# Window attention with group normalisation: each block of x read once into a ring, three transposes per tile

## The chip, the cores and the metric

The kernel runs on one core of one Trainium2 chip. The metric is the device time of one execution in microseconds (us); the median of the runs is compared. The profile is one further execution, recorded instruction by instruction. Engines: TensorE (PE; its weight loads are PEld), VectorE (DVE), ScalarE (ACT), GpSimd (POOL), and SyncE (SP), which here only issues DMAs.

## The reference, cut to what matters

```python
x: (8, 56, 88, 192) float32                      # batch, height, width, channels
def gn(v, G=32, eps=1e-5):                       # 32 groups of 6 channels, per image
    m, s = mean and variance over (height, width, the 6 channels)
    return (v - m) / sqrt(s + eps)
def attn(y):                                     # windows of 7 x 11 = 77 tokens
    qkv = y @ qkv_w + qkv_b                      # 192 -> 576
    q, k, v = 8 heads of 24
    p = softmax(q k^T / sqrt(24))                # 77 x 77 per head and window
    return (p v) @ proj_w + proj_b
return x + attn(gn(x))
```

## The kernel before

**Tiling.** A block is 14 image rows (two strips of windows) by 88 columns: 112 partitions (`PART`, 8 window columns w times 14 rows r), on each 11 tiles (pixel columns c of a window) of 192 channels. There are 32 blocks, four to an image. A block holds 16 windows, worked on as 8 pairs (`PAIRS`), so 256 pairs (`N_PAIRS`). The tiles of a block are spread over its 8 steps as `STEP_TILES`: three steps with two tiles, five with one.

**Precision.** Values are split into a half-precision high and low part. `x_split` holds for each tile four chunks of 128 columns: high of channels 0 to 127; high of channels 128 to 191 twice; low of channels 0 to 127; low of channels 128 to 191 and 64 ones (for the bias). TensorE transposes the four chunks (L826), ScalarE evicts them to `xT` (L439), and five products (`PASSES`, L701) make q, k or v.

**The loop.** All engines run a loop over slots i (`for i in range(FIRST, END)`), written out in full; each engine's order within a slot is the order of the code, and semaphores tie the engines together. In slot i: TensorE computes the scores of pair i (L758), projects the output of pair step i-16 (L721 on), makes v (L713) and k (L706) of pair i+1, adds the row maxima (L793), computes the transposed scores (L744), makes q of pair i+1, transposes the tiles of step i+10 (L826), and multiplies the probabilities of pair i-1 with v (L731). VectorE makes the row maximum (L632), the output with the residual (L640), the low parts q_lo and k_lo, the reciprocal of the denominators (L654), its share of the next image's statistics (`group_stats`, L495), and q_hi (L660). ScalarE evicts the numerators (L433), xT, x_split (L447), v, k_hi, oT_hi, and makes the exponential (L469), which the scores of the next slot wait for. POOL multiplies numerators and reciprocals (L345), normalises the step i+12 (L356, L358), copies and subtracts for the split of step i+11 (L366, L367), makes oT_lo (L371) and, once an image, the power -0.5 of the variances (L336).

**DMAs.** x is read three times: into `x_stat` for the statistics (L252, L290, L391), into `x_norm` for the normalisation (L383, ScalarE's queue), and into `y_blk` for the residual (L283, SP's queue). Blocks are moved in four pieces (`PIECES`), each an access of all 8 window columns and 14 rows. ScalarE loads x_norm and stores the output (L387) at the end of even slots. SP also carries the denominators: out of the numerators (L264), the reciprocals to DRAM (L269), and back, spread over partitions (four DMAs a slot, L276). The loads for the statistics stand in SP's order behind a wait on `stat_read` (L289).

**Statistics.** Image 0 is done in setup on VectorE (L575 to L592). For image g they run in the loop, with the last steps placed by `M1, DEV, SQ, DEV2, M2, ROOT, NEWTON, RSTD` slots ahead of the image.

Of the kernel before, what the change touches and what calls it, by code (L numbers as in the profile page):

```python
# [7 lines left out]
F16 = mybir.dt.float16  # L8
# [23 lines left out]
TILES = WIN_W  # L32
# [14 lines left out]
STAT_PIECES = [(0, 6), (6, 5)]  # L47
# [10 lines left out]
V_BUFS, NUM_BUFS, DEN_BUFS, INV_BUFS, ROW_BUFS = 4, 8, 4, 4, 8  # L58
# [4 lines left out]
A_HI, B_HI2, A_LO, B_LO1 = range(4)  # L63
STAT = 512 - 4 * GROUPS
HI2, LO, ONE = CH, CH + CB, 2 * CH + CB
# [18 lines left out]

M1, DEV, SQ, DEV2, M2, ROOT, NEWTON, RSTD = 21, 20, 19, 18, 17, 16, 15, 14
# [7 lines left out]
def window_attention(nc, x, qkv_w, qkv_b, proj_w, proj_b, out):  # L93
    x_rows = x.rearrange("b (s r) (w c) d -> (b s) (r w) (c d)", r=ROWS, c=WIN_W)
# [4 lines left out]
    with ExitStack() as ctx:  # L99
# [10 lines left out]
        wA, wB, wB_lo = sb("wA", [CA, 3 * CH]), sb("wB", [128, 3 * CH]), sb("wB_lo", [128, 3 * CH])  # L110
# [11 lines left out]
        x_stat = [sb(f"x_stat{h}", [PART, HALF, CH]) for h in range(2)]  # L122
# [6 lines left out]
        x_norm = [sb(f"x_norm{p}", [PART, TILES, CH]) for p in range(2)]  # L129
        x_split = [sb(f"x_split{p}", [PART, TILES, 4 * CA], F16) for p in range(2)]  # L130
        y_blk = [sb(f"y_blk{p}", [PART, TILES, CH]) for p in range(2)]
# [30 lines left out]
        act_num, act_oT, act_x = sem("act_num"), sem("act_oT"), sem("act_x")  # L162
# [10 lines left out]
        dma_x = [[sem(f"dma_x{p}_{k}") for k in range(len(PIECES))] for p in range(2)]  # L173
        dma_y = [[sem(f"dma_y{p}_{k}") for k in range(len(PIECES))] for p in range(2)]
        dma_out = [[sem(f"dma_out{p}_{k}") for k in range(len(PIECES))] for p in range(2)]
        dma_stat = [sem(f"dma_stat{p}") for p in range(2)]
# [13 lines left out]
        def piece(buf, k):  # L190
            t0, n = PIECES[k]
            return buf[:, t0:t0 + n, :].rearrange("p c d -> p (c d)")

        def piece_of(rows, c, k):
            t0, n = PIECES[k]
            return rows[c, :, :, t0 * CH:(t0 + n) * CH]

        def stat_landed(g):
            return 16 * (2 * min(g + 1, 2) + 4 * max(g - 1, 0))

        def x_step(bufs, s):
            t0, n = STEP_TILES[s % PAIRS]
            return bufs[parity(s)][:, t0:t0 + n, :]

        def xT_tokens(buf, c):
            return xT[buf][:, :, 0:COLS].rearrange("p k (v c r) -> p k v c r", v=WINS, c=WIN_W)[:, :, :, c, :]
# [4 lines left out]
        def xT_psum(bank, c):  # L211
            at = 4 * c * PART
            return bank[:, at:at + 4 * PART].rearrange("p (k v r) -> p k v r", k=4, v=WINS)
# [23 lines left out]
        def _(sp):  # L237
# [3 lines left out]
            sp.dma_start(bp[:, :], proj_b.rearrange("(a c) -> a c", a=1).broadcast_to([128, CH])).then_inc(dma_w, 16)  # L241
            sp.wait_ge(pool_const, 2)
            p_rows = proj_w.rearrange("(j g d) c -> g d j c", g=NG, d=HD)
            for g in range(NG):
                sp.dma_start(p32[ROW_G * g:ROW_G * g + HD, :, :], p_rows[g, :, :, :]).then_inc(dma_rows, 16)
            b_row = qkv_b.rearrange("(a c) -> a c", a=1)
            for row in (CB, CB + ROW_G):
                sp.dma_start(bias_in[row:row + 1, :], b_row).then_inc(dma_rows, 16)
            for h in range(2):
                sp.wait_ge(stat_read, h + 1)  # L250
                for n in range(2):
# [601 lines left out]
```

## Time and profile before

| | us |
|---|---|
| median of 3 runs | 1517.04 |
| lowest, highest | 1514.28, 1531.82 |
| the profiled execution | 1531.71 |
| its span, first to last instruction | 1529.9 |
| mean granted clock of TensorE in it | 0.971 |
| TensorE busy | 1361.8 (89%) |
| VectorE busy | 1047.8 (68%) |
| ScalarE busy | 1025.4 (67%) |
| POOL busy | 977.4 (64%) |
| DMA data moved | 170.36 MB, mean 111 GB/s |

How to read it: busy times are sums over one engine; the granted clock is the share of TensorE's full clock of 2.4 GHz (0.5 is 1.2 GHz). Matmuls are pipelined, so a busy TensorE need not be at its peak. Idle time of an engine costs only where it delays the chain of work that ends last; in this profile 77% of that chain is TensorE's.

### The profile page before, as it was taken

The page shows a single profiled execution, that of the slowest core. Times are in us where ns is not written, and L with a number is a line of the kernel's source. Part 1 is how long each engine was busy: PE and PEld are TensorE (multiplying, and loading weights), DVE is VectorE, ACT ScalarE, POOL GpSimd, SP SyncE. Part 2 cuts the span into 40 slices and gives each one's busy share as a digit, 9 for nine tenths or more (in the row PEclk, how much of TensorE's full clock was granted, in tenths as well). Part 3 has the DMA queues.
Part 4 walks back from the last instruction along what each step waited for, and adds up shares of the span by engine and source line. Part 5 has one row for each costly group of instructions (what it writes and reads, how often), then busy time and mean ns, then how long its engine had stood idle before and what let it go on. Part 6 is the DMA issues. An engine that isn't in the chain of part 4 may idle for free.

```text
span 1529.9 us, 84594 instructions
## 1 busy us (share of the span) xinstructions
PE 1361.8 (89%) x36832; PEld 1210.0 (79%) x36832; DVE 1047.8 (68%) x2227; ACT 1025.4 (67%) x1912; POOL 977.4 (64%) x1532
## 2 busy tenths in 40 slices
PE   0489899999998999999999989998999989999995
PEld 0377788888887888888888878887888878888884
DVE  5677677677766766777667866777667766666662
ACT  1567677766776677776767766776667666767761
POOL 0546766677665766767667776777667576767433
PEclk9999999999999999999999999999999999999997
DMA  7233344444444444444444443544433333433333
GB/s 211 69 95 88 112 114 129 120 118 124 108 128 100 115 129 104 129 107 132 111 114 134 113 108 108 132 123 116 116 99 97 98 95 89 106 95 93 85 84 105
DMA packets 129892, 170.36 MB, mean 111 GB/s; under 512 B 46898, under 2 KB 101490, under 8 KB 128628
## 3 DMA queue, kind: packets, MB, share of 16 engines
q1 hardware_dynamic: 98292, 100.59, 26.8%
q10 hardware_dynamic: 31232, 64.35, 14.0%
q8 instruction: 293, 4.80, 1.3%
q14 instruction: 75, 0.61, 0.1%
HBM read 132.04 MB, written 31.54 MB: 107 GB/s over the span
## 4 chain that ended last, share of the span: by engine, by line
PE 77%; DVE 8%; issue 6%; ACT 3%; POOL 3%; DMA 2%; SPq 1%; ACTq 0%; POOLq 0%; DVEq 0%
PE ps_a L698 13%; PE ps_b L698 13%; PE ps_q L698 11%; PE ps_k L698 11%; PE ps_a L731 10%; PE ps_s L744 8%; PE ps_s L758 5%; PE ps_k L826 4%; PE ps_q L793 3%; DVE neg_max L632 2%; POOL st_root L336 2%; DVE stat L495 2%; ACT probs L469 1%; DMA bias_in<-in_qkv_b 1%; DVE st_dev L510 1%
## 5 line engine op out<-in xcount | busy, mean ns | idle before, releaser
L632 DVE TENSOR_REDUCE neg_max<-ps_s 77x16 bf16<-77x1232 f32 x256 | 369.6, 1444 | 221.9 <-PE ps_s L758 221.1
L371 POOL TENSOR_TENSOR oT_lo<-o,oT_hi 128x308 f16<-128x308 f32 x256 | 193.7, 756 | 321.1 <-ACT oT_hi L463 321.1
L469 ACT ACTIVATE probs<-ps_s,exp_shift,exp_scale 77x1232 f32<-77x1232 f32 x256 | 349.2, 1364 | 9.9 <-PE ps_s L744 9.1
L731 PE MATMUL ps_a<-probs,v_all 77*32 77x77 f32 x8192 | 200.6, 234 | 41.1 <-issue 39.8
L452 ACT ACTIVATE v_all<-ps_a 77x384 f32<-77x384 f32 x256 | 124.9, 488 | 166.5 <-PE ps_a L698 166.4
L698 PE MATMUL ps_a<-wv_hiA,xT 128*128 128x192 f16 x1024 | 218.7, 253 | 2.5 <-issue 1.8
L345 POOL TENSOR_TENSOR o<-num,inv_all 128x308 f32<-128x308 f32 x256 | 216.2, 845 | 4.7 <-DMA inv_all<-den_dram 4.7
L439 ACT ACTIVATE xT<-ps_k 128x448 f16<-128x448 f16 x347 | 209.5, 642 | 8.9 <-PE ps_k L826 8.9
L731 PEld LDWEIGHTS ps_a<-probs,v_all 77*32 77x32 f32 x8192 | 148.7, 110 | 68.8 <-issue 44.4
L698 PE MATMUL ps_b<-wp_hi,oT_hi 128*112 128x192 f16 x694 | 188.1, 271 | 13.0 <-POOL oT_lo L371 6.8
L433 ACT ACTIVATE num<-ps_a 128x308 f32<-128x308 f32 x256 | 109.3, 427 | 133.0 <-PE ps_a L731 118.6
L698 PE MATMUL ps_k<-xT,wqk_hiA 128*128 128x154 f16 x1024 | 193.5, 236 | 0.0
L698 PE MATMUL ps_q<-xT,wqk_hiA 128*128 128x154 f16 x1024 | 186.0, 235 | 0.4 <-issue 0.3
L645 DVE TENSOR_TENSOR q_lo<-ps_q,q_hi 128x308 f16<-128x308 f32 x256 | 123.1, 481 | 89.4 <-PE ps_q L793 86.4
L649 DVE TENSOR_TENSOR k_lo<-ps_k,k_hi 128x308 f16<-128x308 f32 x256 | 123.1, 481 | 87.6 <-ACT k_hi L458 86.7
L458 ACT ACTIVATE k_hi<-ps_k 128x308 f16<-128x308 f32 x256 | 110.1, 430 | 106.5 <-PE ps_k L698 106.5
L698 PE MATMUL ps_b<-wp_lo,oT_hi 128*112 128x192 f16 x694 | 177.3, 255 | 0.2 <-issue 0.2
L698 PE MATMUL ps_b<-wp_hi,oT_lo 128*112 128x192 f16 x694 | 177.5, 256 | 0.0
L358 POOL TENSOR_TENSOR x_norm<-x_norm,rstd_all 112x384 f32<-112x384 f32 (+1 forms) x248 | 162.7, 656 | 19.4
L367 POOL TENSOR_TENSOR x_split<-x_norm,x_split 112x384 f16<-112x384 f32 (+1 forms) x248 | 170.2, 686 | 0.0
L356 POOL TENSOR_TENSOR x_norm<-x_norm,mean_all 112x384 f32<-112x384 f32 (+1 forms) x248 | 163.2, 658 | 4.1 <-issue 4.1
L366 POOL COPY x_split<-x_split 112x128 f16<-112x128 f16 (+1 forms) x248 | 64.1, 258 | 155.2 <-ACT x_split L447 154.8
(148 smaller groups left out, 3854.9 us busy)
## 6 DMA issues: line engine op xcount, KB each, us to landing
inv_all<-den_dram SPq DMA_DIRECT2D x1024, 38.5 KB
x_stat<-in_x SPq DMA_DIRECT2D x24, 504.0 KB, 6.1
x_norm<-in_x ACTq DMA_DIRECT2D x32, 336.0 KB
x_norm<-in_x ACTq DMA_DIRECT2D x64, 168.0 KB
y_blk<-in_x SPq DMA_DIRECT2D x32, 336.0 KB
y_blk<-in_x SPq DMA_DIRECT2D x64, 168.0 KB
out<-y_blk ACTq DMA_DIRECT2D x32, 336.0 KB
out<-y_blk ACTq DMA_DIRECT2D x64, 168.0 KB
```

The source lines that it names most:

```text
L345: nc.gpsimd.tensor_tensor(o32[o % 2][:, :], num[o % NUM_BUFS][:, :], inv_all[o % INV_BUFS][:, :], ALU.mult)\
L356: nc.gpsimd.tensor_tensor(x4, x4, of_group(mean_all, g, tiles), ALU.subtract).then_inc(pool_centred, 1)
L358: nc.gpsimd.tensor_tensor(x4, x4, of_group(rstd_all, g, tiles), ALU.mult).then_inc(pool_norm, 1)
L367: nc.gpsimd.tensor_tensor(xs[:, :, LO:ONE], x_step(x_norm, x_s), xs[:, :, 0:CH], ALU.subtract)\
L371: nc.gpsimd.tensor_tensor(oT_tokens(oT_lo, o), by_column(o32[o % 2]), oT_tokens(oT_hi, o), ALU.subtract).then_inc(pool_oT, 1)
L439: last = nc.scalar.activation(xT_tokens(parity(x_s), t0 + c), xT_psum(x_bank(x_s), c), ACT.Copy)
L452: nc.scalar.activation(v_all[v % V_BUFS][:, :, 0:HD], ps_a[0:TOK, 0:2 * CH].rearrange("p (h d) -> p h d", d=HD), ACT.Copy)\
L469: nc.scalar.activation(probs[i % 2][:, :, :].rearrange("p g (a n) -> p g a n", a=4), scores(), ACT.Exp, bias=exp_shift[0:TOK, :], scale=ex ...
L632: nc.vector.tensor_reduce(neg_max[:, :, :, HD:HD + 1].rearrange("p a g e -> p g (a e)"), scores(), AXIS.X, ALU.max, negate=True).then_inc( ...
L645: tt(heads(q_lo), heads(ps_q), heads(q_hi), ALU.subtract).then_inc(dve_q, 1)
L698: last = mm(dst, lhsT, rhs, start=first and n == 0, stop=n == len(pairs) - 1, skip_group_check=True)
L731: last = mm(o, v_all[s % V_BUFS][:, HEADS * w + NG * j + g, :], probs[s % 2][:, g, at:at + TOK], start=True, stop=True, skip_group_check=True)
```

## The change

x is loaded once, by window columns, into `x_ring`, a ring of 11 blocks. Statistics, normalisation and residual all read the ring; the output is added in place and stored from it, by columns, the last block by pieces as before. `x_norm` and `x_split` shrink to three buffers of one step each. `x_split` has three chunks of 128: high of channels 0 to 127; high and low of channels 128 to 191; low of channels 0 to 127. The fourth chunk of `xT` has its 64 rows of ones set once in setup, and POOL copies the 64 rows of the high part into it from the second chunk, after ScalarE's eviction. The steps of the statistics move by up to a slot; square and second moments share one. In setup the weights' DMAs are put in another order, and VectorE normalises step by step; POOL's first step waits for it.

```diff
+RING, STEP_BUFS = 11, 3
+LOAD_LEAD = 8 * RING - 27
-V_BUFS, NUM_BUFS, DEN_BUFS, INV_BUFS, ROW_BUFS = 4, 8, 4, 4, 8
+V_BUFS, NUM_BUFS, DEN_BUFS, INV_BUFS, ROW_BUFS = 3, 8, 4, 4, 8
-A_HI, B_HI2, A_LO, B_LO1 = range(4)
+A_HI, B_BOTH, A_LO, B_ONE = range(4)
-        for h, first in ((0, base - 53), (1, base - 37)):
+        for h in range(2):
             for n in range(GROUPS):
-                at = first + n // 2 if g > 1 else (h * GROUPS + n) // 5 - 3
+                at = base - 47 + n // 2 if h == 0 else base - 31 + n // 3
+                if g == 1:
+                    at = (h * GROUPS + n) // 5 - 3
-M1, DEV, SQ, DEV2, M2, ROOT, NEWTON, RSTD = 21, 20, 19, 18, 17, 16, 15, 14
+M1, DEV, SQ, DEV2, M2, ROOT, NEWTON, RSTD = 20, 19, 18, 18, 17, 16, 15, 14
+        def column(c, w):
+            return x_ring[ROWS * w:ROWS * (w + 1), c % RING, :, :].rearrange("p c d -> p (c d)")
+        def ring_step(s):
+            t0, n = STEP_TILES[s % PAIRS]
+            return x_ring[:, s // PAIRS % RING, t0:t0 + n, :]
...
@@ SP
+            def load_x(c, w):
+                sp.dma_start(column(c, w), x_blk[c, w, :, :]).then_inc(dma_x[c % RING], 16)
+            for c in range(BLOCKS_IMG):
+                for w in range(NWC // 2, NWC):
+                    load_x(c, w)
+            sp.wait_ge(dma_x[2], landed(2))
+            for c in range(BLOCKS_IMG, 2 * BLOCKS_IMG):
+                for w in range(NWC):
+                    load_x(c, w)
...
-                c, r = divmod(i - 5, PAIRS)
-                if r % 2 == 0 and 0 <= c < BLOCKS:
...
-                        sp.wait_ge(stat_read, 2 * g + h - 1)
...
+                c, r = divmod(i + LOAD_LEAD, PAIRS)
+                if r < NWC // 2 and 2 * BLOCKS_IMG <= c < BLOCKS:
+                    reach(sp, dma_out[c % RING][r // 2], NWC // 2 * 16 * (c // RING))
+                    load_x(c, 2 * r)
+                    load_x(c, 2 * r + 1)
@@ GpSimd
+                    if n == PAIRS:
+                        pool.wait_ge(dve_x0, PAIRS)
-                    nc.gpsimd.tensor_tensor(x4, x4, of_group(mean_all, g, tiles), ALU.subtract)
+                    nc.gpsimd.tensor_tensor(x4, raw, of_group(mean_all, g, tiles), ALU.subtract)
...
-                    nc.gpsimd.tensor_copy(xs[:, :, HI2:LO], xs[:, :, CA:CH])
-                    nc.gpsimd.tensor_tensor(xs[:, :, LO:ONE], x_step(x_norm, x_s), xs[:, :, 0:CH], ALU.subtract)
+                    minus(xs[:, :, CH:LO_A], xn[:, :, CA:CH], xs[:, :, CA:CH])
+                    minus(xs[:, :, LO_A:], xn[:, :, 0:CA], xs[:, :, 0:CA]).then_inc(pool_x, 1)
+                x_s = i - 1 + X_LEAD
+                if exists(x_s):
+                    pool.wait_ge(act_xT, x_s + 1)
+                    t0, n = STEP_TILES[x_s % PAIRS]
+                    by_tile = xT[parity(x_s)][0:CB, :, 0:COLS].rearrange("p k (v c r) -> p k v c r", v=WINS, c=WIN_W)
+                    nc.gpsimd.tensor_copy(by_tile[:, B_ONE, :, t0:t0 + n, :], by_tile[:, B_BOTH, :, t0:t0 + n, :]).then_inc(pool_xT, 1)
@@ ScalarE
+            for c in range(BLOCKS_IMG):
+                for w in range(NWC // 2):
+                    nc.scalar.dma_start(column(c, w), x_blk[c, w, :, :]).then_inc(dma_x[c % RING], 16)
...
-                c, r = divmod(i + 18, PAIRS)
-                if r % 2 == 0 and 2 <= c < BLOCKS:
-                    load_x(c, r // 2)
+                c, r = divmod(i - P_LAG - PAIRS, PAIRS)
+                if r < NWC // 2 and 0 <= c < BLOCKS - 1:
+                    act.wait_ge(dve_out, PAIRS * (c + 1))
+                    store_column(c, 2 * r)
+                    store_column(c, 2 * r + 1)
@@ VectorE
-                last = nc.vector.bn_stats(stat6[g % 2][:, h, n, :], x_stat[h][:, :, GCH * n:GCH * (n + 1)])
+                a, b = sorted((one % RING, two % RING))
+                last = nc.vector.bn_stats(stat6[g % 2][:, h, n, :], x_ring[:, a:b + 1:b - a, :, GCH * n:GCH * (n + 1)])
...
+            normalise(0)
+            normalise(1)
+            for step in range(2, PAIRS):
+                split_low(step - 2)
+                normalise(step)
...
-                    if r % 2 == 0:
-                        dve.wait_ge(dma_y[parity(r)][r % PAIRS // 2], 16 * (r // PAIRS // 2 + 1))
-                    y = x_step(y_blk, r)
+                    y = ring_step(r)
@@ TensorE
-            PASSES = ((A_HI, "hiA"), (A_HI, "loA"), (A_LO, "hiA"), (B_HI2, "B"), (B_LO1, "Bb"))
+            PASSES = ((A_HI, "hiA"), (A_HI, "loA"), (A_LO, "hiA"), (B_BOTH, "B"), (B_ONE, "Bb"))
+                    reach(pe, pool_xT, min(v // PAIRS * PAIRS + PAIRS, N_PAIRS))
-                        for chunk in range(4):
+                        for chunk in range(3):
```

## Rows read from the trace of the kernel before

**Rows 1.** Waits of TensorE, 160 to 1373 us: total, times, longest.
```profile
PE ps_a L731 <- issue: 35.6, 25, 3.7
PE ps_s L758 <- ACT probs L469: 12.0, 7, 2.1
```
**Rows 2.** The same view, 1379 to 1486 us; this is its only line.
```profile
PE ps_s L758 <- ACT probs L469: 1.4, 7, 0.2
```
**Rows 3.** Timeline of VectorE, four row maxima (slots 16, 232, 240, 248): start, duration.
```profile
159.52 1.45 DVE L632 TENSOR_REDUCE neg_max<-ps_s 77x16 bf16<-77x1232 f32 x1 [3.51 <-PE ps_s L758]
...
1373.39 1.44 DVE L632 TENSOR_REDUCE neg_max<-ps_s 77x16 bf16<-77x1232 f32 x1 [3.39 <-PE ps_s L758]
...
1415.68 1.44 DVE L632 TENSOR_REDUCE neg_max<-ps_s 77x16 bf16<-77x1232 f32 x1 [0.86 <-PE ps_s L758]
...
1456.16 1.44 DVE L632 TENSOR_REDUCE neg_max<-ps_s 77x16 bf16<-77x1232 f32 x1 [0.73 <-PE ps_s L758]
```
**Rows 4.** Busy time by stretches; last three: granted clock, DMA share, GB/s.
```profile
160.00:1373.00 1213.00, 1137.64 (x31056) 1016.71 (x31054) 847.57 (x1752) 852.83 (x1592) 835.32 (x1303) 0.98 0.43 113
1379.60:1486.00 106.40, 104.85 (x3000) 93.87 (x2992) 73.62 (x127) 74.81 (x136) 55.83 (x89) 1.00 0.36 89
```
**Rows 5.** The same view: start of an odd slot, then two stretches of setup.
```profile
624.60:628.35 3.75, 3.75 (x105) 3.49 (x106) 2.93 (x6) 2.82 (x7) 2.22 (x6) 1.00 0.54 163
22.00:28.00 6.00, 0.00 (x0) 0.00 (x0) 5.86 (x28) 0.00 (x0) 0.39 (x1) 1.00 0.53 196
7.00:14.00 7.00, 0.00 (x0) 0.00 (x0) 0.00 (x0) 0.00 (x0) 0.00 (x0) 1.00 1.03 281
```
**Rows 6.** Timeline, 622 to 631 us: an x_norm load's issue and a TensorE pause.
```profile
622.94 0.70 ACTq L383 DMA_DIRECT2D x_norm<-in_x  x1
...
630.72 0.47 PE L731 MATMUL ps_a<-probs,v_all 77*32 77x77 f32 x16 [1.75 <-issue]
```
**Rows 7.** The page's DMA queues, the instruction queue: packets, MB, share.
```profile
q8 instruction: 293, 4.80, 1.3%
```
**Rows 8.** Timeline of TensorE: scores that begin two slots, transposes of two and one tile.
```profile
456.56 0.32 PE L758 MATMUL ps_s<-k_hi,q_hi 25*128 25x77 f16 x16
460.35 0.56 PE L826 MATMUL ps_k<-ident,x_split 112*128 112x112 f16 x8
461.51 0.32 PE L758 MATMUL ps_s<-k_hi,q_hi 25*128 25x77 f16 x16
...
628.34 0.36 PE L826 MATMUL ps_k<-ident,x_split 112*128 112x112 f16 x4
...
1471.75 0.32 PE L758 MATMUL ps_s<-k_hi,q_hi 25*128 25x77 f16 x16 [0.20 <-ACT probs L469]
...
1476.59 0.32 PE L758 MATMUL ps_s<-k_hi,q_hi 25*128 25x77 f16 x16 [0.20 <-ACT probs L469]
```
**Rows 9.** Groups by shape, POOL: busy us, mean ns, idle before.
```profile
L367 POOL TENSOR_TENSOR x_split<-x_norm,x_split 112x192 f16<-112x192 f32 x155 | 85.1, 549 | 0.0
L367 POOL TENSOR_TENSOR x_split<-x_norm,x_split 112x384 f16<-112x384 f32 x93 | 85.1, 915 | 0.0
L366 POOL COPY x_split<-x_split 112x64 f16<-112x64 f16 x155 | 36.9, 238 | 100.7 <-ACT x_split L447 100.4
```
**Rows 10.** Timeline of VectorE around second moments (slots 110, 111), and the square.
```profile
683.56 0.78 DVE L515 TENSOR_TENSOR st_sq<-st_dev 112x128 f32<-112x128 f32 x1
...
688.39 1.23 DVE L519 SCALAR_TENSOR_TENSOR st_dev<-st_sq,stat 112x64 f32<-112x64 f32 x2
689.54 1.43 DVE L632 TENSOR_REDUCE neg_max<-ps_s 77x16 bf16<-77x1232 f32 x1
```
**Rows 11.** Timeline of VectorE in setup: its first reduction.
```profile
21.71 0.35 DVE L559 TENSOR_REDUCE big_parts<-wA 128x1 f32<-128x192 f32 x1 [15.74 <-DMA bias_in<-in_qkv_b]
```
**Rows 12.** Waits of SP's queue: total, times, longest.
```profile
SPq L290 <- DVE stat L495: 24.9, 1, 24.9
```
**Rows 13.** The chain that ended last, in the tail: a load issued by SP.
```profile
1496.80 0.73 SPq L283
```

More of the change, by code:

```diff
@@ L127, in window_attention @@
         st_dev, st_sq = sb("st_dev", [PART, 2, GROUPS, 2]), sb("st_sq", [PART, 2, GROUPS, 2])
-        x_norm = [sb(f"x_norm{p}", [PART, TILES, CH]) for p in range(2)]
-        x_split = [sb(f"x_split{p}", [PART, TILES, 4 * CA], F16) for p in range(2)]
-        y_blk = [sb(f"y_blk{p}", [PART, TILES, CH]) for p in range(2)]
+        x_ring = sb("x_ring", [PART, RING, TILES, CH])
+        x_norm = [sb(f"x_norm{p}", [PART, 2, CH]) for p in range(STEP_BUFS)]
+        x_split = [sb(f"x_split{p}", [PART, 2, 3 * CA], F16) for p in range(STEP_BUFS)]
         xT = [sb(f"xT{p}", [128, 4, COLS + PAD], F16) for p in range(2)]
@@ L172, in window_attention @@
         dma_inv_all = [sem(f"dma_inv_all{p}") for p in range(INV_BUFS)]
[L173 to L176, printed above, removed]
+        dma_x = [sem(f"dma_x{p}") for p in range(RING)]
+        dma_out = [[sem(f"dma_out{p}_{k}") for k in range(2)] for p in range(RING)]
+        dma_last = sem("dma_last")
         dma_w, dma_rows, dma_bias = sem("dma_w"), sem("dma_rows"), sem("dma_bias")
@@ L240, in _ @@
             sp.dma_start(wB[CB:128, :], qkv_w[CA:CH, :]).then_inc(dma_w, 16)
-            sp.dma_start(bp[:, :], proj_b.rearrange("(a c) -> a c", a=1).broadcast_to([128, CH])).then_inc(dma_w, 16)
             sp.wait_ge(pool_const, 2)
+            b_row = qkv_b.rearrange("(a c) -> a c", a=1)
+            for row in (CB, CB + ROW_G):
+                sp.dma_start(bias_in[row:row + 1, :], b_row).then_inc(dma_rows, 16)
             p_rows = proj_w.rearrange("(j g d) c -> g d j c", g=NG, d=HD)
@@ L245, in _ @@
                 sp.dma_start(p32[ROW_G * g:ROW_G * g + HD, :, :], p_rows[g, :, :, :]).then_inc(dma_rows, 16)
[L246 to L251, printed above, removed]
-                    sp.dma_start(x_stat[h][:, n * TILES:(n + 1) * TILES, :].rearrange("p c d -> p (c d)"),
-                                 x_rows[BLOCKS_IMG + 2 * h + n, :, :]).then_inc(dma_stat[h], 16)
+            sp.dma_start(bp[:, :], proj_b.rearrange("(a c) -> a c", a=1).broadcast_to([128, CH])).then_inc(dma_w, 16)
+            def load_x(c, w):
[7 more added lines that the diff above has]
+                    load_x(c, w)
             sp.wait_ge(dve_bp, 1)
@@ L305, in _ @@
                                     base=0, pattern=[[-1, 128]], channel_multiplier=1).then_inc(pool_const, 1)
-            for p in range(2):
-                nc.gpsimd.memset(x_split[p][:, :, ONE:], 1.0)
             pool.wait_ge(weights_big, 1)
@@ L492, in group_stats @@
             def group_stats(g, h, n):
+                one, two = BLOCKS_IMG * g + 2 * h, BLOCKS_IMG * g + 2 * h + 1
                 if n == 0:
-                    dve.wait_ge(dma_stat[h], stat_landed(g))
-                last = nc.vector.bn_stats(stat6[g % 2][:, h, n, :], x_stat[h][:, :, GCH * n:GCH * (n + 1)])
+                    dve.wait_ge(dma_x[one % RING], landed(one))
+                    dve.wait_ge(dma_x[two % RING], landed(two))
+                a, b = sorted((one % RING, two % RING))
+                last = nc.vector.bn_stats(stat6[g % 2][:, h, n, :], x_ring[:, a:b + 1:b - a, :, GCH * n:GCH * (n + 1)])
                 if n == GROUPS - 1:
```

130 lines of the change are left out of this document (48 added, 82 removed).

## The prediction

> **What bounds the kernel now.** I read the waits of TensorE first, then the starts of one recurring instruction, then busy time by stretches, then single instructions. The loop handles one pair of windows per slot, 256 slots.
>
> TensorE's waits from 160 to 1373 us [rows 1] are mostly "issue": time in which it waited for no engine, 35.6 us inside the attention product alone. In a later stretch the only wait left is 1.4 us for the exponential [rows 2]. The two stretches run the same loop. The starts of VectorE's row maximum give the price [rows 3]. Slots 16 to 232 (27 blocks of eight) take 1373.39 - 159.52 = 1213.9 us, 44.96 us a block. The block from slot 240 takes 1456.16 - 1415.68 = 40.5 us. So the middle loses 27 x 4.46, about 120 us, against a pace that the same engines keep later. The granted clock says the same [rows 4]: 0.98 against 1.00.
>
> What ended near 1373 us? ScalarE's loads into x_norm (L383) stop, after slot 236. Even before, each even slot ended with two DMAs on ScalarE's queue, a load and a store. Their data moves in the following odd slot [rows 5]: the first row is the first 3.75 us of an odd slot, DMA share 0.54. The second row is a stretch of setup with x_norm loads alone: 0.53 and 196 GB/s, flat. The third has the statistics' long rows and reaches 1.03 and 281 GB/s. So the block-shaped DMAs occupy about half of the 16 engines and hold those for long. An example of the cost [rows 6]: the load is issued at 622.94, and TensorE stands still 1.75 us in the attention product ending at 630.72, "issue". The instruction queue fetches 293 packets, 4.80 MB, 16 KB each [rows 7], about one per 4.6 us, which is TensorE's own code. In the packet records the fetches of TensorE's code that come late all start in odd slots. **My reading:** a fetch waits behind the x burst on its DMA engine; TensorE runs dry; after long pauses it resumes at 1.2 GHz for a while.
>
> The Trainium skill ("DMA: Bandwidth & Descriptors", section "Why a DMA increments its semaphore by 16 and not by 1") says a DMA from SP or ACT uses the largest k up to 16 dividing the slowest dimension on both sides. For x_norm, y_blk and out that dimension is 8 in DRAM, so k = 8; by that rule, the 0.53 agrees. For the new column DMAs of 14 rows it gives 14.
>
> **The change, part by part**, against the profiled execution's own 1531.7 us (span 1529.9 and 1.8 around it).
>
> 1. *x traffic.* Three reads of x become one; loads and stores become columns of 14 rows of 8448 bytes, two per slot: stores in slots 0 to 3 of a block, loads in slots 3 to 6. A slot then moves 236 KB, where an odd slot now moves 420 to 504 KB from ScalarE's queue and 168 to 336 KB from SP's. Of the 120 us, two parts are no fetches: POOL's power instruction delays the exponential once an image (12.0 us in seven waits, [rows 1], and an estimated 8 more for the 1.2 GHz stretch that follows the pause), and VectorE's statistics steps some 8 us. About 91 us remain. The later stretch has stores and y loads only, 336 KB or less per burst, and loses nothing. The new bursts are smaller still. Bounds: 0 saved (bursts are not the cause) and 91. I take 79, leaving 12. **-79 us.**
>
> 2. *Three transposes per tile.* In a two-tile slot eight transposes take 0.56 and in a one-tile slot four take 0.36 [rows 8], so 0.05 each. But one-tile slots gain nothing: between 1471.75 and 1476.59 no transposes are left, TensorE waits 0.20 us for the exponential, and the slot still is 4.84 us, as it is with four. There the exponential ends last. A slot with eight transposes, 456.56 to 461.51, takes 4.95, 0.11 above that bound, so two fewer save the whole 0.096. 91 x 0.096: **-9 us** (bounds 0 and 352 x 0.05 = -18). ScalarE's shorter eviction (336 for 448 columns) is followed by idle time in the slot: nothing.
>
> 3. *POOL.* Old per step: copy 0.24 for 64 elements, subtraction 0.55 for 192, 0.92 for 384 [rows 9], so 1.9 ns an element above 0.18 fixed. New: two subtractions, 0.31 + 0.43 for one tile, 0.43 + 0.67 for two, and the copy out of the transposed chunk, 112 or 224 half-precision elements on 64 partitions. No row has this copy; bounds 0.24 and 0.18 + 224 x 1.9 ns = 0.61, I take 0.28 and 0.38, near the old copy, whose kind it is. POOL's busiest slots come to 4.8 us with all its work, inside slots of 4.83 to 4.96. It covers itself, and its late product has 2.7 us of slack before ScalarE needs it. Cover gone: 0.5 us in 31 blocks. The copy waits for ScalarE's eviction, which comes in the same slot earlier than the x_split POOL waits for already; behind it only oT_lo is queued. TensorE's new wait for the copy, once a block at the v projection, is met a slot before: **0.**
>
> 4. *Statistics.* Square and second moments share one slot now. VectorE's second moments (1.23 us) already make the next row maximum late: it starts 0.65 after the scores instead of 0.37 [rows 10]. Adding 0.78 for the square puts this whole amount on the path, seven times (bounds 0 and twice this, should the clock fall): **+6.** Three group statistics per slot instead of two in eleven slots add 0.21 before q_hi, whose slack before the next scores is 0.23 by the starts in the trace: 0.
>
> 5. *Setup.* VectorE's first reduction waits until 21.71 us for the bias rows [rows 11], which share the engines with 5.5 MB of x. Now 1.9 MB stand beside the weights. At 281 GB/s [rows 5], 2.7 MB take 9.7 us; with 2 us of start and 2 of landing, 14.5. Statistics then find blocks 0 and 1 landed. **-7** (0 to -10). POOL must now wait with the second block's three two-tile steps (two instructions each, near the 0.92 of [rows 9]) until VectorE is done, though VectorE itself finishes earlier: **+2** (-2 to +5). The extra memsets sit in the idle 15 us.
>
> 6. *SP's early wait.* SP stood 24.9 us behind the statistics before a load [rows 12], so the first denominators came late and slots 4 and 5 stretched by 3 us. Gone: **-3** (0 to -3). SP's new waits are for stores issued two slots before; behind them stand the denominators, with about 8 us of slack. Its issue work in the loading slots is 2.6 us + two columns at 0.3 to 0.73: under 4.1 of 4.8.
>
> 7. *Tail.* No y load between the last denominators, 0.73 each [rows 13]: **-2** (0 to -5). ScalarE issues two column stores where it issued a load and a store: 0.
>
> Sum: -79 - 9 + 6 - 7 + 2 - 3 - 2 = -92, so 1440 us. The median of the runs is 1517, about 15 below the profiled run; I hold that this is a lighter share of the same stalls, which vanish anyway (64 instead of 79). That gives 1517 - 77 = **1440** too.
>
> **Rivals.**
>
> *The idle is not the bursts.* Then only parts 2 to 7 count: -13, **1504 us.** For it: the fetch packets themselves are short even at stalls, so what I call a queue is a start that comes late, and no row shows what it queued behind. Against: rows 2 and 3. The Trainium skill ("Runtime: NRT & Kernel Launch", section "Instruction fetch mechanics") holds that crossing a 16 KB boundary is mostly hidden; by it this rival is the likely case. The trace speaks against: 35.6 us of pauses. Chance 0.12.
>
> *Half of it.* Bursts in seven slots of eight, with 8448-byte packets, still make some fetches late: 35 to 40 us stay instead of 12, **1466 us.** Chance 0.14.
>
> *Slower: every slot gets a burst.* If a fetch is held by the size of the packets before it and not by the burst's length, late fetches move from half of the slots to seven eighths, and today's 91 us become 160: 1504 + 69 = **1573 us.** It decides from the point where one slot's 236 KB hold a fetch about 2 us or more. Against it: setup's 8448-byte rows move at 281 GB/s, so 236 KB are through in 1 us. Chance 0.05.
>
> *POOL's copy costs its upper bound or more,* late at block borders: +15, **1455.** Inside the forecast's case.
>
> **From cases to numbers.** Forecast 0.69, 1425 to 1460. A measurement of this kernel can tell about 2% from no change, 30 us: faster is below 1487, slower above 1547. Faster: 0.69 + 0.14, less some scatter, 0.81. Same: the first rival and scatter, 0.13. Slower 0.06. The range goes from 1418 (all of 91 saved, setup at its bound) to 1492, leaving out the first rival and the slower one.
>
> **What would show it.** "Issue" waits of TensorE under 15 us; clock 0.99 or more in the middle; blocks of about 41 us throughout; a first reduction near 14.5 us; the one-tile slot still 4.83; POOL's busy time up about 60 us with no wait for it; the slot after the second moments 0.8 longer. Wrong it would be if "issue" stays at 50 us with the DMA share lower.

## The result and the profile after

The changed kernel takes 1452.31 us (median of 4 runs, 1450.42 to 1455.38) against 1520.55 for the kernel before beside it (4 runs, 1514.28 to 1531.82): a ratio of 0.9545, 95% interval 0.9483 to 0.9608. It is faster; the prediction was 1440, in a range of 1418 to 1492. A median is over all runs of a kernel and a ratio over those within 1.5% of its fastest, so beside the widely scattered kernel before of 1525.22 us, below, the two do not divide out. The profiled execution has a span of 1450.9 us against 1529.9, 79.0 less.

The page: span, busy time by engine, DMA queues, HBM.

```profile
span 1450.9 us, 84355 instructions
...
PE 1321.5 (91%) x36480; PEld 1174.7 (81%) x36480; DVE 1049.3 (72%) x2239; ACT 987.0 (68%) x1910; POOL 1027.8 (71%) x1786
...
q10 hardware_dynamic: 7872, 32.18, 12.6%
q8 instruction: 291, 4.77, 1.4%
...
HBM read 71.49 MB, written 31.54 MB: 71 GB/s over the span
```

TensorE's code is still 4.8 MB in some 290 fetches, as in [rows 7]. The queue q10, on which ScalarE's DMAs run, carries 32 MB: the stores and 1.9 MB of x in setup, without the loads of x_norm. The waits of TensorE from 160 to 1373 us (total, times, longest) answer to [rows 1]:

```profile
PE ps_s L757 <- ACT probs L464: 16.0, 11, 2.3
PE ps_q L793 <- DVE neg_max L633: 6.2, 17, 0.6
PE ps_s L743 <- issue: 2.3, 8, 0.4
PE ps_k L826 <- issue: 1.2, 3, 0.6
PE ps_a L730 <- issue: 1.0, 3, 0.5
```

"Issue" summed over all lines of this view was 56.0 us before and is 6.3 now. What is left at the top is the wait for the exponential, which POOL's power delays (halving the power, below, takes it from 16.0 to 5.7). Busy time by stretches (last three: granted clock, DMA share, GB/s), as in [rows 4]:

```profile
160.00:1373.00 1213.00, 1176.95 (x32826) 1052.42 (x32823) 899.80 (x1848) 874.21 (x1695) 929.05 (x1609) 0.99 0.36 75
```

In the same 1213 us TensorE does 32,826 matmuls where it did 31,056. The row maxima of slots 16, 232, 240 and 248, as in [rows 3] (timeline of VectorE: start, duration, idle before):

```profile
155.89 1.44 DVE L633 TENSOR_REDUCE neg_max<-ps_s 77x16 bf16<-77x1232 f32 x1 [0.35 <-PE ps_s L757]
...
1295.49 1.45 DVE L633 TENSOR_REDUCE neg_max<-ps_s 77x16 bf16<-77x1232 f32 x1 [0.76 <-PE ps_s L757]
...
1336.37 1.44 DVE L633 TENSOR_REDUCE neg_max<-ps_s 77x16 bf16<-77x1232 f32 x1 [0.76 <-PE ps_s L757]
...
1376.86 1.44 DVE L633 TENSOR_REDUCE neg_max<-ps_s 77x16 bf16<-77x1232 f32 x1 [0.73 <-PE ps_s L757]
```

The middle takes 1139.6 us in 27 blocks, 42.21 a block where it was 44.96. The late block takes 40.49, as before.

To say where the 79.0 us came from, I give each slot a floor, the 15th percentile of the slots with the same place in a block, and call the rest its excess. Before to after, profiled runs:

| stretch | before | after | difference | predicted |
|---|---|---|---|---|
| to the scores of slot 0 | 71.9 | 74.3 | +2.4 | -5 |
| floors of slots 0 to 254 (40.54 to 40.21 a block) | 1292.3 | 1281.9 | -10.4 | -9 |
| excess, slots 0 to 15 | 6.1 | 0.8 | -5.3 | -3 |
| excess, slots 16 to 231 | 119.4 | 53.9 | -65.5 | -73 |
| excess, later slots | 1.7 | 1.6 | 0 | 0 |
| last scores to the end | 38.6 | 38.4 | -0.2 | -2 |
| sum | 1529.9 | 1450.9 | -79.0 | -92 |

### The profile page after: what moved, and what is told of

Read it like the earlier page. It is cut to its first block, busy times and chain, and to the rows that moved or that the text cites. A ratio compares the mean times of both kernels' runs of the same rounds, so it can differ in the third digit from the quotient of the medians.

```text
span 1450.9 us, 84355 instructions
## 1 busy us (share of the span) xinstructions
PE 1321.5 (91%) x36480; PEld 1174.7 (81%) x36480; DVE 1049.3 (72%) x2239; ACT 987.0 (68%) x1910; POOL 1027.8 (71%) x1786
## 4 chain that ended last, share of the span: by engine, by line
PE 77%; DVE 10%; POOL 4%; ACT 3%; issue 3%; DMA 2%; SPq 1%; ACTq 0%; POOLq 0%; DVEq 0%
PE ps_a L697 13%; PE ps_b L697 13%; PE ps_q L697 12%; PE ps_k L697 11%; PE ps_a L730 9%; PE ps_s L743 8%; PE ps_s L757 5%; DVE neg_max L633 3%; PE ps_q L793 3%; PE ps_k L826 3%; POOL st_root L331 3%; ACT probs L464 2%; DVE stat L495 2%; DMA x_ring<-in_x 1%; DVE q_hi L659 1%
## 5 line engine op out<-in xcount | busy, mean ns | idle before, releaser
L313 POOL TENSOR_TENSOR x_split<-x_norm,x_split 112x128 f16<-112x128 f32 (+1 forms) x496 | 205.8, 436 | 67.1 <-ACT x_split L442 66.8
L697 PE MATMUL ps_a<-wv_hiA,xT 128*128 128x192 f16 x1024 | 213.2, 248 | 6.5 <-ACT num L428 3.4
L730 PE MATMUL ps_a<-probs,v_all 77*32 77x77 f32 x8192 | 194.6, 233 | 1.5 <-issue 1.4
L697 PE MATMUL ps_b<-wp_hi,oT_hi 128*112 128x192 f16 x694 | 184.1, 265 | 13.0 <-POOL oT_lo L373 7.5
L697 PE MATMUL ps_b<-wp_hi,oT_lo 128*112 128x192 f16 x694 | 173.3, 250 | 0.1
L697 PE MATMUL ps_b<-wp_lo,oT_hi 128*112 128x192 f16 x694 | 173.2, 250 | 0.0
L434 ACT ACTIVATE xT<-ps_k 128x336 f16<-128x336 f16 x347 | 168.3, 524 | 5.3 <-PE ps_k L826 5.3
L352 POOL TENSOR_TENSOR x_norm<-x_ring,mean_all 112x384 f32<-112x384 f32 (+1 forms) x248 | 161.5, 651 | 1.4 <-DVE x_split L613 1.4
L458 ACT ACTIVATE oT_hi<-o 128x308 f16<-128x308 f32 x256 | 117.6, 459 | 27.7 <-POOL o L340 27.7
```

The lines of the kernel that those rows point to most:

```text
L313: return nc.gpsimd.tensor_tensor(out, a, b, ALU.subtract)
L352: nc.gpsimd.tensor_tensor(x4, raw, of_group(mean_all, g, tiles), ALU.subtract).then_inc(pool_centred, 1)
L434: last = nc.scalar.activation(xT_tokens(parity(x_s), t0 + c), xT_psum(x_bank(x_s), c), ACT.Copy)
L697: last = mm(dst, lhsT, rhs, start=first and n == 0, stop=n == len(pairs) - 1, skip_group_check=True)
L730: last = mm(o, v_all[s % V_BUFS][:, HEADS * w + NG * j + g, :], probs[s % 2][:, g, at:at + TOK], start=True, stop=True, skip_group_check=True)
```

## The experiments

Two theories of the 56 us of issue waits stood after the result. **T** (the prediction's): the x traffic in flight at once holds TensorE's code fetches. **Q**: what holds them is two transfers back to back on ScalarE's one queue, a load of x_norm and a store, whatever the other queues move; the ring removes this pair because its loads are SP's. Q came up during the first experiments, whose expectations do not name it. In the kernel before, ScalarE issues the load 0.74 us before the store (median of 108 pairs in the timeline). Behind the load of [rows 6] at 622.94 comes:

```profile
623.68 0.69 ACTq L387 DMA_DIRECT2D out<-y_blk  x1
```

So the pair is close in two ways, on one queue and in time, and an edit can change both at once. The first two kernels start from the one before.

**The load of x_norm one slot later than the store.**

```diff
-                c, r = divmod(i + 18, PAIRS)
+                c, r = divmod(i + 17, PAIRS)
```

> The kernel before with one number changed: ScalarE issues its x_norm loads at the end of odd slots, no longer in the same slot as the output's stores. Bytes, sizes and all other instructions are the same. Theory (TensorE's code fetches wait behind the x bursts, and a burst of load plus store is too long): the load now meets SP's y load and the store stands alone, so the longest burst is shorter; the idle called issue falls from 56 us to 10 to 35, the time to 1460 to 1500. Rival one (it is the amount of x traffic that counts): no change, 1512 to 1525. Rival two (the idle has nothing to do with these DMAs): no change either.

Measured: 1483.63 us, ratio to before 0.9679 (0.9616 to 0.9741); issue waits 21.3 us in all. Not a byte less is moved, and 48 us are gone, inside the range of the first theory. So the number of bytes is not it; how they meet is. T and Q both expect this.

**No load of x_norm at all.** Blocks 2 to 31 are normalised from what lies in the buffer; the reading of x for that is left out, and POOL's waits for it.

```diff
...
-                c, r = divmod(i + 18, PAIRS)
-                if r % 2 == 0 and 2 <= c < BLOCKS:
-                    load_x(c, r // 2)
```

> The kernel before without the x_norm loads of blocks 2 to 31: it leaves out reading x for the normalisation, so those blocks normalise what is already in the buffer; all engine instructions stay. Theory: what remains are store bursts and y loads as in the later stretch of before that lost nothing, so issue idle falls under 15 us and the time by 60 to 90 us, to 1430 to 1460. Rival one (amount of traffic): x traffic falls by a quarter, so at most a quarter of the loss goes, 1495 to 1505. Rival two (not these DMAs): 1512 to 1525.

Measured: 1472.90 us, 0.9596 (0.9538 to 0.9655); issue waits 17.3 us. That is 59 us less, little more than moving the load gave, and above the 1430 to 1460 that the theory expected.

**The old shape in the new kernel.** Loads by SP and stores by ScalarE are the old four pieces, in even slots; `load_piece` is the old access into the ring.

```diff
-                if r < NWC // 2 and 2 * BLOCKS_IMG <= c < BLOCKS:
-                    reach(sp, dma_out[c % RING][r // 2], NWC // 2 * 16 * (c // RING))
-                    load_x(c, 2 * r)
-                    load_x(c, 2 * r + 1)
+                if r % 2 == 0 and 2 * BLOCKS_IMG <= c < BLOCKS:
+                    reach(sp, dma_out[c % RING][r // 4], 2 * 16 * (c // RING))
+                    load_piece(c, r // 2)
...
```

> The changed kernel with its in-loop loads and stores in the old form: four pieces a block over all 8 window columns, one load by SP and one store by ScalarE in each even slot, into and out of the ring. x is still read once and the bytes are those of the changed kernel. Theory (the shape and length of the burst count): 500 KB bursts on half of the DMA engines are back in one slot of two, issue idle rises from about 10 us to 30 to 60 and the time by 30 to 70 us, to 1480 to 1520. Rival one (the amount, three reads against one, counts): as the changed kernel, 1448 to 1458.

Measured: 1459.38 us, 0.952 (0.9465 to 0.9575); issue waits 10.5 us. With pieces as long as before, in every second slot, the stalls stay away, and the 30 to 60 us of the theory are missed. The columns' shape is not what helps in the loop. But the burst of load and store is not back as it was: SP issues its load a median of 3.2 us after ScalarE's store, as here:

```profile
617.05 0.67 ACTq L391 DMA_DIRECT2D out<-x_ring  x1
619.92 0.74 SPq L253 DMA_DIRECT2D x_ring<-in_x  x1
```

**The same, with the loads on ScalarE's queue.** Only the slot numbers and the call are shown.

```diff
-                c, r = divmod(i + 66, PAIRS)          # in SP's loop
-                    load_piece(c, r // 2)
+                c, r = divmod(i + 66, PAIRS)          # in ScalarE's loop, ahead of the store
+                    load_piece(c, r // 2)
```

> The changed kernel, but each block's load and store are both issued by ScalarE's queue, back to back in the same even slot, as the old four pieces. Against the run before it (loads by SP, stores by ScalarE, the same pieces in the same slots, 1459 us) only the queue of the loads is different; the bytes are the same. Theory Q (two transfers on ScalarE's one queue hold up what comes behind them, TensorE's program fetches among it): the code stalls come back, issue waits of 20 to 45 us between 160 and 1373 us, 1480 to 1510 us. Theory T (what counted is the x traffic in flight at once, of which the ring leaves two thirds out): the same as with SP's loads, 1455 to 1465 us, issue waits under 12 us.

Measured: 1485.24 us, 0.969 (0.9641 to 0.974), with the unedited changed kernel on the same chip at 1461.87. Waits of TensorE, 160 to 1373 us:

```profile
PE ps_s L742 <- issue: 11.6, 8, 2.8
...
PE ps_k L825 <- issue: 4.1, 5, 1.8
PE ps_q L696 <- issue: 3.8, 2, 2.2
```

28.5 us of issue in all, single pauses of up to 2.8 us. Same bytes, same pieces, same slots of the program: 23 us more than the changed kernel. The time and the issue waits lie in Q's ranges and not in T's. Half of the old stalls come back, not all. But the queue is not all that changed. The load is now issued 0.74 us before the store (median of 87 pairs):

```profile
624.51 0.70 ACTq L381 DMA_DIRECT2D x_ring<-in_x  x1
625.25 0.69 ACTq L387 DMA_DIRECT2D out<-x_ring  x1
```

So this run shows that the pair makes stalls, and not whether by its one queue or by its two bursts falling together.

**The changed kernel again.** No edit.

> The changed kernel once more, unedited, so that the others can be set against it on one chip. All theories: 1452 us (1446 to 1462), a ratio to before of 0.950 to 0.958, issue waits of TensorE of some 6 us in all between 160 and 1373 us.

Measured: 1461.87 us (1457.21 to 1465.37), 0.9531 (0.948 to 0.9583); issue waits 7.0 us. On this chip both kernels run longer, by 1.1% and 0.7%; the ratio is the same within its interval.

**The kernel before, without the loads of y_blk.** VectorE's waits for them go too; the output of blocks 2 to 31 adds what lies in the buffer.

```diff
-                if r % 2 == 0 and 0 <= c < BLOCKS:
+                if r % 2 == 0 and 0 <= c < 2:
...
```

> The kernel before, with the loads of y_blk taken out for blocks 2 to 31, which leaves out re-reading x for the residual of those blocks (they add what lies in the buffer). ScalarE's queue keeps only the stores, SP keeps the loads of x_norm and x_stat. Theory Q (load and store back to back on ScalarE's queue): the pair is gone, stalls fall as with the loads alone removed elsewhere or more, 1450 to 1475 us. Theory T (total traffic at once): x_norm's load in the same slots was worth 47 to 59 us when moved or left out, and y_blk's is as large, so 1465 to 1490 us. If instead only SP's load in the slots of ScalarE's pair mattered (theory S), nothing changes: 1515 to 1530 us.

Here I had named the queues wrongly. y_blk is loaded by SP, in odd slots; x_norm and the store are ScalarE's pair, and this kernel keeps that pair whole. What I wrote for Q and S rests on that mix-up, and that the time fell in S's range says nothing. Read rightly, Q expects the stalls to stay. T's sentence stands: a load as large is gone, 1465 to 1490 us. Measured: 1516.74 us, 0.9899 (0.9845 to 0.9953). Waits of TensorE, 160 to 1373 us:

```profile
PE ps_a L732 <- issue: 29.4, 24, 2.5
...
PE ps_s L759 <- issue: 3.8, 3, 2.0
PE ps_k L827 <- issue: 3.1, 3, 2.3
```

43.1 us of issue in all. To leave out y_blk is worth 1%, to leave out x_norm, as many bytes, 4%. T's range is missed, and bytes per slot are not the measure. In the kernel before, y_blk's load is issued a median of 3.1 us ahead of the store; the pair is what this kernel keeps, close in time and on one queue.

**The kernel before, with the loads of x_norm on SP's queue.** Same slots of the program, same bytes; ScalarE's three lines go.

```diff
                 # SP, behind the load of y_blk
+                c, r = divmod(i + 18, PAIRS)
+                if r % 2 == 0 and 2 <= c < BLOCKS:
+                    k = r // 2
+                    if c == 2:
+                        sp.wait_ge(dve_x0, 2 * k + 2)
+                    reach(sp, pool_x, PAIRS * (c - 3) + 2 * k + 2)
+                    sp.dma_start(piece(x_norm[c % 2], k), piece_of(x_blk, c, k)).then_inc(dma_x[c % 2][k], 16)
```

> The kernel before, with one edit: the loads of x_norm are issued by SP's queue instead of ScalarE's, in the same even slots; bytes, pieces and buffers stay, ScalarE's queue keeps the stores. Theory Q (a load and a store back to back on ScalarE's queue hold up TensorE's program fetches): few late fetches are left, issue waits under 20 us between 160 and 1373 us, 1470 to 1490 us. Theory T (the x traffic in flight at once counts, on whatever queue): stalls stay, issue waits of 45 to 65 us, 1515 to 1535 us.

Measured: 1484.05 us (1471.96 to 1500.44), with a widely scattered kernel before beside it (1525.22, 1494.39 to 1551.21), so 0.9846 (0.9702 to 0.9989). Its profile is of the fastest of its four runs. Waits, then the stretch:

```profile
PE ps_s L748 <- issue: 3.9, 4, 1.9
PE ps_a L735 <- issue: 3.7, 6, 1.4
PE ps_s L762 <- issue: 3.2, 4, 1.6
```

```profile
160.00:1373.00 1213.00, 1177.37 (x32743) 1055.13 (x32742) 887.15 (x1826) 900.28 (x1679) 875.28 (x1374) 0.99 0.47 118
```

13.6 us of issue in all, at 118 GB/s, more than the 113 of [rows 4]. All the traffic is there, and TensorE does 32,743 matmuls in the stretch, nearly the changed kernel's 32,826. The median and the issue waits lie in Q's ranges, and neither the traffic as a whole nor its rate makes the stalls. Whether it is the queue, this run does not say either, because the load has moved in time as well: a median of 3.5 us behind the store.

```profile
617.76 0.67 ACTq L394 DMA_DIRECT2D out<-y_blk  x1
622.74 0.73 SPq L290 DMA_DIRECT2D x_norm<-in_x  x1
```

The stalls that remain speak for time. In the three kernels without the pair, SP still issues x_stat loads of 420 to 504 KB, and 21 stores in each have one within 2 us. In the 7 us behind such a store TensorE has 0.47, 0.27 and 0.45 us of issue (load moved by a slot, on SP's queue, left out); behind the other 91 or 92 stores it has 0.06, 0.04 and 0.06. These are two queues, which suggests that one queue is not needed for a stall. The changed kernel has no such loads. On the other side, y_blk's smaller loads do little even when they are the nearest and within 1 us: 0.09 us behind 15 stores. This is counted from the timelines, not tested by an edit. An SP load issued right beside the store would part T, in the narrow form of two bursts at once, from Q; it was not run.

**Four transposes in the changed kernel.** `x_split` has its fourth chunk again, and POOL copies within `x_split` as before.

```diff
-                        for chunk in range(3):
-                            at = (3 * c + chunk) * PART
+                        for chunk in range(4):
+                            at = (4 * c + chunk) * PART
...
```

> The changed kernel with the fourth chunk transposed again by TensorE and evicted by ScalarE, and POOL copying the 64 high columns inside x_split; everything else as changed. Theory: the three transposes save only in the two-tile slots, so going back costs 91 times 0.1, 9 us: 1460 to 1463. Rival (all 352 transposes lie on the path, at 0.05 each): 18 us, 1470. Second rival (POOL's copies out of the transposed chunk cost more than they save): no change or faster, 1445 to 1453.

Measured: 1458.23 us, 0.951 (0.9454 to 0.9566), the same ratio as the changed kernel's within the interval, and between the ranges that I had given. The floor goes back to 40.54 a block, but the excess of slots 16 to 231 is 49.3 us where the changed kernel has 53.9 and, in its second run, 56.4. So of 10.4 us that three transposes take off the floors, no more can be seen in the total than the scatter of these runs.

**Statistics apart.**

```diff
-                at = base - 47 + n // 2 if h == 0 else base - 31 + n // 3
+                at = base - 48 + n // 2 if h == 0 else base - 32 + n // 3
-M1, DEV, SQ, DEV2, M2, ROOT, NEWTON, RSTD = 20, 19, 18, 18, 17, 16, 15, 14
+M1, DEV, SQ, DEV2, M2, ROOT, NEWTON, RSTD = 21, 20, 19, 18, 17, 16, 15, 14
```

> The changed kernel, but its statistics are read one slot earlier and square and second moments stand in slots of their own, as in the kernel before. Theory (the shared slot costs 0.8 us seven times): 5 to 7 us less than the changed kernel, 0.5% at most. Rival (another wait in that slot hides it): within 2 us of it.

Measured: 1452.45 us, 0.9666 (0.9598 to 0.9734; the scattered kernel before of this chip stands in the ratio). The excess of the five slots with statistics, summed over the six images whose statistics lie between slots 16 and 231, is 12.1 us, against 13.7 and 13.3 in the changed kernel's two runs: 1 to 2 us, so the rival is right. The timelines of VectorE show a difference that fits; the changed kernel first, this one second:

```profile
655.04 0.84 DVE L515 TENSOR_TENSOR st_sq<-st_dev 112x128 f32<-112x128 f32 x1
655.91 0.61 DVE L519 SCALAR_TENSOR_TENSOR st_dev<-st_sq,stat 112x64 f32<-112x64 f32 x2
656.45 1.43 DVE L633 TENSOR_REDUCE neg_max<-ps_s 77x16 bf16<-77x1232 f32 x1
```

```profile
650.49 0.85 DVE L515 TENSOR_TENSOR st_sq<-st_dev 112x128 f32<-112x128 f32 x1
...
655.31 1.30 DVE L519 SCALAR_TENSOR_TENSOR st_dev<-st_sq,stat 112x64 f32<-112x64 f32 x2
656.54 1.43 DVE L633 TENSOR_REDUCE neg_max<-ps_s 77x16 bf16<-77x1232 f32 x1
```

Behind the square the second moments take 0.61 us; alone in a slot they take 1.30. Square and moments make 1.45 together, not the 2.0 of [rows 10] that I had added up.

**The power in two halves.** POOL does 16 of the 32 groups in each of two slots; VectorE's step behind it waits for both.

```diff
-M1, DEV, SQ, DEV2, M2, ROOT, NEWTON, RSTD = 20, 19, 18, 18, 17, 16, 15, 14
+M1, DEV, SQ, DEV2, M2, ROOT, NEWTON, RSTD = 20, 19, 18, 18, 17, 16, 14, 13
-                nc.gpsimd.tensor_tensor(st_root[:, :], st_var[:, :], half_power[:, :], ALU.pow).then_inc(pool_root, 1)
+                nc.gpsimd.tensor_tensor(st_root[:, half], st_var[:, half], half_power[:, half], ALU.pow).then_inc(pool_root, 1)
...
```

> The changed kernel, but POOL's power -0.5 of the variances, 5.4 us in one instruction once an image, is done in two halves in two successive slots, and what follows it stands one slot later. Theory (the power delays POOL's late product and with it ScalarE's numerators and exponential; slots 17 and 18 of an image now cost 24 us over their floor in all seven images, and a half of 2.7 us fits into the slack): 18 to 24 us less than the changed kernel, 1434 to 1442 us where that has 1458, and the waits of TensorE's scores for the exponential fall from 16 us to under 4. Rival (a half still breaks the chain, now in two slots): 0 to 8 us less.

Measured: 1464.26 us, 0.9726 (0.9635 to 0.9818). A miss: no gain, and 12 us more than the kernel with the statistics apart that ran beside it. The exponential's waits do fall, from 16.0 to 5.7 us, but a new one takes their place. Waits of TensorE, 160 to 1373 us, and then VectorE and POOL in the slot behind the second half:

```profile
PE ps_q L795 <- DVE neg_max L635: 19.9, 22, 2.1
PE ps_s L759 <- ACT probs L466: 5.7, 9, 0.9
```

```profile
512.98 3.22 DVE L537 TENSOR_TENSOR newton<-st_root 112x32 f32<-112x32 f32 x1
516.23 0.56 DVE L538 TENSOR_TENSOR newton<-newton,st_var 112x32 f32<-112x32 f32 x1
516.83 1.44 DVE L635 TENSOR_REDUCE neg_max<-ps_s 77x16 bf16<-77x1232 f32 x1
```

```profile
514.10 0.76 POOL L374 TENSOR_TENSOR oT_lo<-o,oT_hi 128x308 f16<-128x308 f32 x1
514.82 0.84 POOL L341 TENSOR_TENSOR o<-num,inv_all 128x308 f32<-128x308 f32 x1
515.62 0.52 POOL L353 TENSOR_TENSOR x_norm<-x_ring,mean_all 112x192 f32<-112x192 f32 x1
516.23 0.52 POOL L355 TENSOR_TENSOR x_norm<-x_norm,rstd_all 112x192 f32<-112x192 f32 x1
```

A product of 112x32 elements, 0.19 us in setup, takes 3.22 (3.02 to 3.31 in the seven images) while POOL, catching up after its half, works without a pause; it ends as POOL passes from one instruction to the next. The row maximum stands behind it. VectorE's small step in another slot is the next thing to try; it was not run.

**Blocks 0 to 3 loaded as pieces.** 112 partitions in one transfer, blocks 0 and 1 by ScalarE, 2 and 3 by SP.

```diff
-                for w in range(NWC // 2):
-                    nc.scalar.dma_start(column(c, w), x_blk[c, w, :, :]).then_inc(dma_x[c % RING], 16)
+                for k in range(len(PIECES)):
+                    nc.scalar.dma_start(ring_piece(c, k), block_piece(c, k)).then_inc(dma_x[c % RING], 16)
...
```

> The changed kernel, but the first four blocks are loaded as pieces of several window columns (112 partitions in one transfer) instead of 16 columns each of 14 partitions; blocks 0 and 1 by ScalarE's queue, 2 and 3 by SP's. Theory: the columns reach only 148 GB/s in the setup against 196 GB/s for pieces in the kernel before, so VectorE's first statistics, which start at 27.7 us now, start at 21 to 24 us and everything moves up with them: 4 to 6 us less than the changed kernel, 1446 to 1448 us where that has 1452. Rival: the first statistics are held by the reduction of the weights and by HBM shared among all loads, whatever their shape: within 1.5 us of the changed kernel.

Measured: 1457.08 us, 0.9494 (0.9443 to 0.9546), on the chip where the changed kernel had 1461.87 and 0.9531. Setup in the timeline of VectorE and by stretches, the changed kernel first and then this one:

```profile
18.04 0.35 DVE L561 TENSOR_REDUCE big_parts<-wA 128x1 f32<-128x192 f32 x1 [9.14 <-DMA bp<-in_proj_b]
...
27.73 2.47 DVE L495 BATCH_NORM_STATS2 stat<-x_ring 112x6 f32<-112x132 f32 x12 [5.72 <-DMA x_ring<-in_x]
```

```profile
10.00:18.00 8.00, 0.00 (x0) 0.00 (x0) 0.00 (x0) 0.00 (x0) 0.00 (x0) 1.00 0.92 148
```

```profile
11.73 0.35 DVE L569 TENSOR_REDUCE big_parts<-wA 128x1 f32<-128x192 f32 x1 [2.84 <-DMA bp<-in_proj_b]
```

```profile
10.00:18.00 8.00, 0.00 (x0) 0.00 (x0) 3.82 (x15) 0.00 (x0) 0.39 (x1) 1.00 0.52 200
```

Columns keep the DMA engines 0.92 busy and move 148 GB/s; pieces keep them 0.52 busy and move 200. The statistics start at 21.1 us, and the first scores come at 68.4, where the changed kernel had 74.3 and 73.7. The theory holds in the setup, 5 to 6 us. At the end it can't be told from scatter: the medians differ by 4.8 us, the profiled spans, 1455.0 and 1455.4, by 0.4.

**All three.** Statistics apart, power halved, pieces in setup.

> The changed kernel with three edits together: statistics one slot earlier with square and second moments apart, the power in two halves, and the first four blocks loaded as pieces of several window columns. If the three add up (5, 20, 5): 1425 to 1432 us where the changed kernel has 1458, a ratio to before of 0.930 to 0.936. If the fetches turn late at other places for it, or the halves do not fit: 1440 to 1452 us.

Measured: 1455.45 us (6 runs, 1452.36 to 1461.72), 0.9685 (0.9629 to 0.9741). This is above both ranges, 3 us above the second, whose case it is: the halves do not fit. Slots 18 to 20 of the images hold 27 us of excess, where in the changed kernel slots 17 and 18 hold 24. The gain of setup is within the scatter of the total, so no version here beats the changed kernel by what these runs can tell.

## Why the prediction was right, and where its reason was not

**Step 1, -79 of -92.** The place was right: TensorE's issue waits in the middle, 56.0 us, fell to 6.3, and the excess with them; -65.5 against the -73 of this step and step 4 together. The mechanism was half wrong. "A fetch waits behind the x burst on its DMA engine" took all x traffic of a slot for one burst, and the argument that a new slot moves less made bytes per slot the measure. The runs show that the load of x_norm, issued by ScalarE 0.74 us ahead of its store, is the cause of most stalls: moved by a slot, moved to SP's queue (and so away from the store) or left out, it leaves 21.3, 13.6 and 17.3 us; y_blk on SP's queue, as large and 3.1 us ahead of the store, could go and 43.1 stayed. Two bursts at once or two transfers on one queue: the runs do not part these, and the remaining stalls near x_stat loads speak for the first. [Rows 5] had suggested that pieces take half of the engines and hold those for long. They do, and with the load 3.2 us from the store it costs little (10.5 us of issue). That the late block was clean with stores and y loads fits both theories; I took it for mine. Why the pair delays a fetch of another queue no row shows; it stays open, as does the half of the stalls that the pair did not bring back in the changed kernel.

The Trainium skill ("Runtime: NRT & Kernel Launch", section "Instruction fetch mechanics") calls the crossing of a 16 KB boundary mostly hidden. The changed kernel agrees (6.3 us in some 290 fetches) and the kernel before does not (56.0 us in as many): crossing the boundary is hidden in the one and was not where a load and a store were issued back to back. My first rival, which rested on it, is out.

The rival "half of it" gave 1466 with 35 to 40 us of stalls staying. 6.3 us stayed, so the profile is not in its case; the excess that I had put at 12 + 20 + 8 us ended at 53.9: POOL's power takes 24.3 instead of 20 (slots 17 and 18 of the seven images), the statistics 13.7, and 16 are spread thinly.

**Step 2, -9.** The floors fell by 10.4. The three slots of a block in which two tiles are transposed went from 4.95, 5.01 and 5.45 to 4.86, 4.88 and 5.35; the others stayed at 4.83 and 5.32, as [rows 8] implied. In the timeline of TensorE a one-tile slot, from 603.84 to 608.67, and the six transposes of the slot behind it:

```profile
603.84 0.32 PE L757 MATMUL ps_s<-k_hi,q_hi 25*128 25x77 f16 x16
...
608.67 0.32 PE L757 MATMUL ps_s<-k_hi,q_hi 25*128 25x77 f16 x16
612.46 0.46 PE L826 MATMUL ps_k<-ident,x_split 112*128 112x112 f16 x6
```

Whether it reaches the end the run with four transposes can't show: its total differs from the changed kernel's by less than the runs scatter.

**Step 3, 0.** POOL's busy time rose by 50 us where I had said 60, and no wait of TensorE for POOL came between 160 and 1373 us. The copy took 0.30 us for one tile (mean of 160) and 0.38 for two, where I had taken 0.28 and 0.38. Its row, and that of the subtractions of 128 elements, 0.43 as expected:

```profile
L370 POOL COPY xT<-xT 64x112 f16<-64x112 f16 x160 | 48.1, 301 | 2.8 <-ACT xT L434 2.8
L313 POOL TENSOR_TENSOR x_split<-x_norm,x_split 112x128 f16<-112x128 f32 x248 | 106.2, 428 | 24.0 <-ACT x_split L442 23.9
```

**Step 4, +6.** It came to 1 to 2: behind the square the second moments take 0.61 us and not the 1.23 of [rows 10]. POOL is busy beside both, and which of its instructions stretches them no run tested.

**Step 5, -7 + 2.** The step that failed: it came to +2.4. I took 281 GB/s from [rows 5], the rate of long rows over 112 partitions, for columns of 14 partitions; they move 148. So the first reduction came at 18.04 instead of 14.5, and the statistics waited again, 5.72 us, until 27.73, where before they had begun at 25.58. POOL's chain cost 0.3, not 2.

**Step 6, -3,** gave -5.3 by the table. Slots 4 and 5 gave 3.0 of it, as forecast; most of the rest is a pause in issue of 2.6 us at the end of slot 15, which belongs to step 1. **Step 7, -2,** gave -0.2: with the load away, TensorE's wait in the tail for POOL's oT_lo grew from 6.8 to 7.5 us. The load was on the chain [rows 13]; without it the chain runs in the last slots from POOL's o to ScalarE's oT_hi and POOL's oT_lo, and the tail is as long.

The slower rival fell: seven slots of eight carry a burst, and fetches are on time.

The misses offset each other in part. In the profiled runs the change is 13 us short of the forecast, 7.4 of it in setup, 7.5 in the middle and 1.8 in the tail, less 3.7 by which the floors and the first slots gave more than their terms. Between the medians it is 68 us against 77.

## What to carry to other kernels

When TensorE pauses in "issue", look at which large loads and stores are issued within a microsecond or two of each other, on one queue above all, and try one of them a slot off or on another queue before rebuilding the data flow: here an edit of one line brought 3.2% where the ring with all its parts brought 4.5%. When an edit moves a DMA to another queue, read from the timeline when it is now issued: here the queue and the time changed together, and that left the mechanism open. Take the rate of a DMA from a row with the same number of partitions, not the same row length. And price a small VectorE step by what POOL does in that slot.

## What the runs showed of the hardware

- A small product of VectorE's with both operands in SBUF lengthens beside POOL: 0.19 us in setup, 0.67 in the changed kernel's loop, 3.22 beside an unbroken row of POOL's. The Trainium skill ("SBUF — State Buffer", section "SBUF: two separate sides") says that VectorE and GpSimd share a pair of ports under an exclusive lock, taken for a whole instruction; the rows fit this and add that the product did not get in between several of POOL's.
- POOL's power takes 5.44 us for 112x32 elements and 2.90 for 112x16.
- In setup, columns of 14 partitions and 8448 bytes each keep 0.92 of the DMA engines busy for 148 GB/s; pieces of 112 partitions keep 0.52 busy for 200.
- In the changed kernel the granted clock fell to 1.2 GHz 7.5 to 9.2 us after the start of five of the seven powers, for 3.4 us (once 6.8), TensorE having waited 2.2 to 2.3 us for the exponential just before. Over the whole span it stood at 1.2 GHz for 88 us in the kernel before and 37 in the changed one.
